# Attention streams of four groups: VectorE copies fills 0 and 1 of a round, ScalarE fills 2 and 3

## The chip, the cores and the metric

The kernel runs on one NeuronCore of a Trainium2 chip. The metric is the device time of one execution in microseconds (us); the time before is the median of three runs. A separate execution was recorded by the hardware profiler; all durations below come from it. PE is TensorE's matmul queue, PEld its weight loads, DVE is VectorE, ACT is ScalarE, POOL is GpSimd.

## The reference

The program is a stack of four pairs of an attention layer and a feed-forward layer over x of 8 x 256 x 256 (fp32), each normed first. Three of the four attention layers are touched. Cut to what they compute, per batch b of eight and head h:

```python
s = q[b, h] @ k[b, h].T (+ mask)      # 256 queries x keys
p = exp(s - max(s, axis=-1))
o = (p @ v[b, h]) / p.sum(-1)
x[b] += concat(o over h) @ Wp + bias
```

- ra (layer 0): 16 heads of 16, 256 keys, a mask of two classes and five register tokens that are treated on their own.
- ca (layer 1): 16 heads of 16, 512 keys (256 of the context, 256 of x itself).
- ma (layer 3): 8 heads of 32, 256 keys, masked.

## The kernel before, in words

All attention layers run through one generator, `attention_stream`. A stream is cut into rounds n = 0, 1, ... (NR of them, R for each batch). In a round four score units u = 0 to 3 are made, each a 128 x 512 block (128 queries by one head with 512 keys, or two heads with 256) in PSUM bank u. ra has 32 rounds, ca 64 (R = 8), ma 16 (R = 2). For each round:

- TensorE computes the four units (`scores`, L664; ra and ma add a mask product first, L660). Unit u may only be overwritten when ScalarE has taken the exponentials of the same unit of the round before (`exped`).
- VectorE takes the row maximum of each unit (`maxima`, L872). ScalarE takes the exponential of each (`exps`, L806) into prob. Where a unit has two heads, that is two exponentials.
- In the next round TensorE transposes prob (`turn(n-1, f)`, L678): a fill f is four 128 x 128 transposes that fill one PSUM bank. There are four fills in a round and two banks: fills 0 and 2 go to bank 4, fills 1 and 3 to bank 5. A fill is copied from PSUM to SBUF (pT) by `copy_turned`, on ScalarE L814, on VectorE L878. turn(., 2) waits until fill 0 has been copied, turn(., 3) until fill 1 has, turn(., 0) and turn(., 1) until fills 2 and 3 of the round before have.
- In every second round (odd n from 3) TensorE multiplies the transposed values of two rounds with v into bank 7 (`values`, L702).
- Other uses share bank 6, one after the other, at set places of a round: the projections of the next batch (front: L1187, L1203, in ma L1743, L1756, L1770), the output projection (L1161, L1791), the spread of the inverse sums (L721, copied by ScalarE at L828 and used by VectorE in `scale`, L900), in ra the register tokens (L745 to L760, with VectorE's L920 and ScalarE's L822).

Each engine has its own program, written out in full, and executes it in its order; engines meet only at semaphores. Nothing is reordered by a scheduler: the order of the calls in this function is the order on each engine. TensorE's order within a round n is

```
scores(n); shared slot 0; turn(n-1,0); turn(n-1,1); values or shared slot 1;
turn(n-1,2); turn(n-1,3); shared slot 1 if there were values; shared slot 2
```

and the change leaves it as it is. In ca the shared uses all lie in slot 1: fronts and output projection in even rounds between turns 1 and 2, the spread in rounds n%8 = 1 behind turn 3. `FILLS` is the number of fills in a round: 4 for ra, ca and ma (four groups), 2 for the streams na and pa, which keep their code.

Of the kernel before, what the change touches and what calls it, by code (L numbers as in the profile page):

```python
# [503 lines left out]
def attention_stream(g, ctx, tag, heads, dh, groups, keys, front, front_at, q_of, k_of, v_of, slot_of, project, finish,  # L504
# [12 lines left out]
    NR = B * R  # L517
# [4 lines left out]
    FILLS = NB  # L522
# [40 lines left out]
    def local(h):  # L563
        return h % HF

    def unit(n, u):
        r = n % R
        return (r % 2, u, groups[r // 2][u]) if GA == 4 else (u // 2, u % 2, groups[r][u % 2])

    def values_due(n):  # L570
        return 2 <= n <= NR + 1 and (n - 2) % VR == VR - 1
# [21 lines left out]
    def freer(use):  # L593
        if use[0] == "front":
            return front[use[2]][0]
        if use[0] == "reg":
            return ("a", "v", "v", "v")[use[2]]
        return {"project": "v", "spread": "a", "null": "a", "null_product": "v"}[use[0]]
# [15 lines left out]
    def shared_bank(use):  # L614
        n = ready_at[use] - 1
        return g.bank[n % 4] if n < len(first) else M

    with nc.Block() as block:
        @block.sync
        def _(sp):  # L620
            if n_loads:
                for b in range(B):
                    if b >= 2:
                        load_after(sp, b - 2, ready, ready_at, valued, R)
                    for d in load(sp, b):
                        d.then_inc(ld[b % 2], 16)
            sp.wait_ge(wl, 16 * n_weights)
# [16 lines left out]
        def _(pe):  # L644
# [24 lines left out]
            def turn(n, f):  # L669
                fill = FILLS * n + f  # L670
                last = f if NB == 4 else 2 * f + 1
                pe.wait_ge(exped, 4 * n + last + 1)
                if fill >= 2:
                    pe.wait_ge(copied_v if f % 2 == 0 else copied_a, (fill - 2) // 2 + 1)
                for j in range(4):
                    u, blk = (f, j) if NB == 4 else (2 * f + j // 2, j % 2)
                    c0 = (blk // KC) * keys + (blk % KC) * P
                    mm = pe.transpose(TB[f % 2][:, j * P:(j + 1) * P], prob[:, n % 2, u, c0:c0 + P], ident)  # L678
                mm.then_inc(turned, 1)
# [114 lines left out]
        @block.scalar  # L794
        def _(act):
            act.wait_ge(wl, 16 * n_weights)

            def exps(n, u):
                i, a, hs = unit(n, u)
                f = n // RF  # L800
                act.wait_ge(maxed, 4 * n + u + 1)
                if null is not None and n >= 2:
                    act.wait_ge(null_taken, n - 1)
                for hh in range(per):
                    hl = local(hs[hh])
                    e = act.activation(prob[:, n % 2, u, hh * keys:(hh + 1) * keys],  # L806
                                       S[u][:, hh * keys:(hh + 1) * keys], ACT.Exp, bias=nmax[:, n % 2, u, hh:hh + 1],
                                       accum_out=sums[:, f % 2, i, hl:hl + 1])
                e.then_inc(exped, 1)

            def copy_turned(n, f):
                act.wait_ge(turned, FILLS * n + f + 1)
                o = pT[:, n // 2 % 2, 4 * f:4 * f + 4, n % 2] if GA == 4 else pT[:, n % 2, :, f]
                act.activation(o, TB[f % 2][:].rearrange("p (j q) -> p j q", j=4), ACT.Copy).then_inc(copied_a, 1)  # L814

            def shared(use):
                if freer(use) != "a":
                    return
                bank = shared_bank(use)
                if use[0] == "reg":  # L820
                    act.wait_ge(reg_maxed, use[1] + 1)
                    e = act.activation(rp[:], bank[0:RN, 0:N], ACT.Exp, bias=rst[:, 0:1], accum_out=rst[:, 1:2])  # L822
                else:
                    act.wait_ge(ready, ready_at[use])
                    if use[0] == "front":
                        e = front[use[2]][2](act, bank, use[1])
                    elif use[0] == "spread":
                        e = act.activation(spreadS[:, use[1] % 2], bank[:], ACT.Copy)  # L828
                    else:
                        e = act.activation(pnT[:], bank[0:heads, 0:N], ACT.Copy)  # L830
                e.then_inc(freed_a, 1)

            for use in first:
                shared(use)
            for n in range(NR + 3):
                if n < NR:
                    exps(n, 0)
                    exps(n, 1)
                for use in slots[n][0]:
                    shared(use)  # L840
                if FILLS == 4:
                    if 1 <= n <= NR:
                        copy_turned(n - 1, 1)
                    if n < NR:
                        exps(n, 2)
                        exps(n, 3)
                    if not values_due(n):
                        for use in slots[n][1]:
                            shared(use)
                    if 1 <= n <= NR:  # L850
                        copy_turned(n - 1, 3)
                    if values_due(n):
                        for use in slots[n][1]:
                            shared(use)
                else:
                    if n < NR:
                        exps(n, 2)
                        exps(n, 3)
                    if 1 <= n <= NR:
                        copy_turned(n - 1, 1)  # L860
                    for use in slots[n][1]:
                        shared(use)
                for use in slots[n][2]:
                    shared(use)

        @block.vector
        def _(v):
            v.wait_ge(wl, 16 * n_weights)

            def maxima(n, u):  # L870
                v.wait_ge(scored, 4 * n + u + 1)
                v.tensor_reduce(nmax[:, n % 2, u], S[u][:, 0:W].rearrange("p (h k) -> p h k", h=per),  # L872
                                AX.X, ALU.max, negate=True).then_inc(maxed, 1)

            def copy_turned(n, f):
                v.wait_ge(turned, FILLS * n + f + 1)
                o = pT[:, n // 2 % 2, 4 * f:4 * f + 4, n % 2] if GA == 4 else pT[:, n % 2, :, f]
                v.tensor_copy(o, TB[f % 2][:].rearrange("p (j q) -> p j q", j=4)).then_inc(copied_v, 1)  # L878
# [28 lines left out]
            def reg_queries(b):  # L907
                wait_front(v, b)
                v.tensor_tensor(rq0[:], reg["q"](0, b), reg["q"](1, b), ALU.add).then_inc(reg_made, 1)
                v.wait_ge(reg_made, 3 * b + 1)  # L910
                for k in range(KD):
                    v.tensor_tensor(rq[:, k], rq0[:, k].unsqueeze(1).to_broadcast([P, 16, REG]),
                                    g.c("head16")[:, 16 * k:16 * k + 16].unsqueeze(2).to_broadcast([P, 16, REG]),
                                    ALU.mult).then_inc(reg_made, 1)
# [29 lines left out]
                shared(use)  # L944
            for n in range(NR + 3):
                if n < NR:
                    for u in range(2 if FILLS == 4 else 4):
                        maxima(n, u)
                    if reg is not None and n % R == 0:
                        reg_queries(n // R)  # L950
                for use in slots[n][0]:
                    shared(use)
                if 1 <= n <= NR:
                    copy_turned(n - 1, 0)
                if FILLS == 4:
                    if n < NR:
                        maxima(n, 2)
                        maxima(n, 3)
                    if not values_due(n):
                        for use in slots[n][1]:  # L960
                            shared(use)
                    if 1 <= n <= NR:
                        copy_turned(n - 1, 2)
                    if values_due(n):
                        for use in slots[n][1]:
                            shared(use)
                else:
                    for use in slots[n][1]:
                        shared(use)
                for use in slots[n][2]:  # L970
                    shared(use)
                if 1 <= n <= NR and (n - 1) % RF == RF - 1:
                    invert((n - 1) // RF)
                if 2 <= n <= NR + 1 and (n - 2) % RF == RF - 1:
                    scale((n - 2) // RF)
# [1272 lines left out]
```

## Time and profile before

| what | value |
|---|---|
| median of three runs | 2984.89 us (2981.12 to 2985.41) |
| the profiled execution, its time | 2986.86 us |
| its span in the profile | 2985.1 us |
| PE busy | 2450.5 us, 82% |
| DVE busy | 1213.5 us, 41% |
| ACT busy | 1049.7 us, 35% |
| ra stream, about | 290 to 566 us |
| ca stream, about | 600 to 953 us |
| ma stream, about | 2316 to 2512 us |

The span is the time between the first and the last recorded instruction; the execution's own time is 1.8 us longer. The streams that the diff touches take some 825 us of it. Busy shares are of the whole program, whose stages have different limits, so each stream has to be read for itself.

### The profile page before, as it was taken

To read this page: it belongs to the slowest core of one execution; us is meant where nothing else is said; L and a number is where in the kernel's file an instruction comes from. 1 tells how busy PE (TensorE), PEld (TensorE's weight loads), DVE (VectorE), ACT (ScalarE), POOL (GpSimd) and SP (SyncE) were. 2 spreads that over 40 slices of the span, in tenths; PEclk is the share of its full clock that TensorE was granted. 3 is DMA by queue.
4 is the path that set the end of the run, shared out by engine and by line. 5 is a ranking of instruction groups with operands and counts; after the bars stand their busy time and mean duration, and the time that the engine had idled before them with its cause. 6 is when DMAs were issued, how large, how long until landed. Compare 5 with 4: busy or idle time off the path is not lost. (4 is left out here: it accounts for less than half of the span.)

```text
span 2985.1 us, 39248 instructions
## 1 busy us (share of the span) xinstructions
PE 2450.5 (82%) x15064; PEld 1672.4 (56%) x15064; DVE 1213.5 (41%) x2325; ACT 1049.7 (35%) x2908; POOL 268.3 (9%) x323
## 2 busy tenths in 40 slices
PE   2464888789997589889899999997998997884894
PEld 2231556556665344444666666665786666664673
DVE  4234666577776221222333333334543444222003
ACT  1311556467775112221233333334321443322211
POOL 0000000000000123223000000002001000002003
PEclk9686999999999799999999999999999999887897
DMA  1100000000000200000200000000001000003332
GB/s 52 51 15 2 1 1 1 29 19 22 12 22 1 85 0 0 0 0 2 105 8 8 8 8 8 1 1 26 1 1 54 29 15 15 1 1 110 117 110 60
DMA packets 51018, 74.71 MB, mean 25 GB/s; under 512 B 8210, under 2 KB 40612, under 8 KB 49444
## 3 DMA queue, kind: packets, MB, share of 16 engines
q1 hardware_dynamic: 49316, 68.20, 6.7%
q0 software_dynamic: 1536, 4.20, 0.5%
q8 instruction: 116, 1.90, 0.3%
q14 instruction: 50, 0.41, 0.0%
HBM read 63.90 MB, written 8.39 MB: 24 GB/s over the span
## 5 line engine op out<-in xcount | busy, mean ns | idle before, releaser
L806 ACT ACTIVATE ca_prob<-bank,ca_nmax 128x512 f32<-128x512 f32 x256 | 174.2, 691 | 93.6 <-DVE ca_nmax L872 93.6
L872 DVE TENSOR_REDUCE ca_nmax<-bank 128x1 f32<-128x512 f32 x256 | 164.0, 682 | 57.0 <-PE bank L664 56.9
L1416 DVE TENSOR_TENSOR rf_hh<-rf_rc,rf_r 128x512 f32<-128x512 f32 x96 | 66.4, 692 | 293.1 <-POOL rf_rc L1322 293.1
L806 ACT ACTIVATE na_prob<-bank,na_nmax 128x257 f32<-128x257 f32 x256 | 118.1, 474 | 180.8 <-DVE na_nmax L872 180.8
L1355 PE MATMUL bank<-rf_xg,rf_W 128*128 128x512 f32 x384 | 179.1, 592 | 0.0
L1348 PE MATMUL bank<-rf_hh,rf_W 128*128 128x512 f32 x384 | 179.1, 592 | 0.0
L806 ACT ACTIVATE ra_prob<-bank,ra_nmax 128x256 f32<-128x256 f32 x256 | 118.4, 484 | 104.0 <-DVE ra_nmax L872 104.0
L678 PEld LDWEIGHTS bank<-cst,ca_prob 128*128 128x128 f32 x1024 | 112.1, 141 | 73.1 <-issue 63.7
L1322 POOL TENSOR_TENSOR rf_rc<-rf_r,rf_cw 128x512 f32<-128x512 f32 x96 | 124.4, 1296 | 286.2 <-ACT rf_r L1377 286.2
L1377 ACT ACTIVATE rf_r<-bank 128x512 f32<-128x512 f32 x96 | 57.3, 597 | 251.7 <-PE bank L1355 251.7
L678 PE MATMUL bank<-cst,ca_prob 128*128 128x128 f32 x1024 | 140.2, 279 | 6.0 <-DVE ca_pT L878 5.2
L872 DVE TENSOR_REDUCE na_nmax<-bank 128x1 f32<-128x257 f32 x256 | 90.8, 417 | 118.2 <-PE bank L664 118.2
L1348 PEld LDWEIGHTS bank<-rf_hh,rf_W 128*128 128x128 f32 x384 | 72.9, 190 | 91.9 <-issue 70.5
L1355 PEld LDWEIGHTS bank<-rf_xg,rf_W 128*128 128x128 f32 x384 | 72.6, 190 | 89.9 <-issue 89.9
L1603 PE MATMUL bank<-sf_h,sf_W 128*128 128x512 f32 x512 | 120.1, 395 | 0.0
L1485 PE MATMUL bank<-na_cxT,na_Wkv 128*128 128x256 f32 x512 | 118.5, 384 | 1.7 <-DVE na_q L1479 0.8
L1497 PE MATMUL bank<-na_Wkv,na_cxT 128*128 128x512 f32 x256 | 116.8, 601 | 3.3 <-ACT na_spread L828 2.6
L1603 PEld LDWEIGHTS bank<-sf_h,sf_W 128*128 128x128 f32 x512 | 95.9, 187 | 23.5
L1485 PEld LDWEIGHTS bank<-na_cxT,na_Wkv 128*128 128x128 f32 x512 | 95.0, 190 | 24.4 <-DVE na_q L1479 6.2
L664 PE MATMUL bank<-ca_k,ca_qz 32*128 32x512 f32 x512 | 73.9, 644 | 26.4 <-ACT ca_prob L806 25.6
L878 DVE COPY ca_pT<-bank 128x512 f32<-128x512 f32 x128 | 87.4, 683 | 16.4 <-PE bank L678 16.4
L237 PE MATMUL bank<-ln_rstd,cst 128*128 128x128 f32 x352 | 51.9, 291 | 49.8 <-DVE ln_rstd L311 49.8
(388 smaller groups left out, 4655.6 us busy)
## 6 DMA issues: line engine op xcount, KB each, us to landing
xl_w<-in_L_ffn_w SPq DMA_DIRECT2D x16, 1024.0 KB
rf_W<-in_L_ffn_w SPq DMA_DIRECT2D x2, 3072.0 KB, 14.4
dp_cx<-in_ctx_tok SPq DMA_DIRECT2D x4, 1024.0 KB, 5.5
ca_v<-in_ctx_values SPq DMA_DIRECT2D x8, 512.0 KB, 4.1
na_Wkv<-in_L_xattn_Wkv SPq DMA_DIRECT2D x1, 4096.0 KB
na_cxT<-in_ctx SPq DMA_DIRECT2D x8, 512.0 KB, 3.5
ma_cxT<-in_ctx SPq DMA_DIRECT2D x8, 512.0 KB, 3.5
X<-in_x SPq DMA_DIRECT2D x1, 2048.0 KB
```

Source lines behind the costliest of these rows:

```text
L664: mm = pe.matmul(S[u][:, hh * keys:(hh + 1) * keys], q_of(hs[hh], i, b), k_of(hs[hh], i, b), start=(mask is None), stop=(hh == per - 1), s ...
L678: mm = pe.transpose(TB[f % 2][:, j * P:(j + 1) * P], prob[:, n % 2, u, c0:c0 + P], ident)
L806: e = act.activation(prob[:, n % 2, u, hh * keys:(hh + 1) * keys], S[u][:, hh * keys:(hh + 1) * keys], ACT.Exp, bias=nmax[:, n % 2, u, hh: ...
L872: v.tensor_reduce(nmax[:, n % 2, u], S[u][:, 0:W].rearrange("p (h k) -> p h k", h=per), AX.X, ALU.max, negate=True).then_inc(maxed, 1)
L878: v.tensor_copy(o, TB[f % 2][:].rearrange("p (j q) -> p j q", j=4)).then_inc(copied_v, 1)
L1322: po.tensor_tensor(rc[:, c % 3], r[:, c % 3], cw[:, expert[c]], ALU.mult).then_inc(rcd, 1)
L1348: mm = pe.matmul(g.bank[6 + m][:], W2[:, c, m * P:(m + 1) * P], hh[:, c % 3], start=(c == 0), stop=(c == CH - 1), skip_group_check=True)
L1355: mm = pe.matmul(g.bank[2 + c % 3][:], W1[:, k, c * P:(c + 1) * P], xg[:, k], start=(k == 0), stop=(k == KD - 1))
L1416: v.tensor_tensor(hh[:, c % 3], rc[:, c % 3], r[:, c % 3], ALU.mult).then_inc(hd, 1)
L1485: mm = pe.matmul(bank[:, m * N:(m + 1) * N], Wkv[:, k, (m0 + m) * P:(m0 + m + 1) * P], cxT[:, b % 2, k], start=(k == 0), stop=(k == KC - 1))
L1497: mm = pe.matmul(bank[:], cxT[:, b % 2, k, t * P:(t + 1) * P], Wkv[:, k, INNER + half * 512:INNER + (half + 1) * 512], start=(k == 0), sto ...
L1603: mm = pe.matmul(g.bank[m % 4][:], W1[:, k, m * P:(m + 1) * P], h[:, k, s], start=(k == 0 and s == 0), stop=(k == C1 - 1 and s == 1))
```

## The change

In streams with four fills VectorE now copies fills 0 and 1, and ScalarE fills 2 and 3; before, VectorE had 0 and 2, ScalarE 1 and 3. VectorE takes three maxima, copies fill 0, takes the fourth maximum and copies fill 1. ScalarE takes all four exponentials in a row, and then copies fills 2 and 3. TensorE's waits are adapted: turns 2 and 3 wait for VectorE's copies of the same round, turns 0 and 1 for ScalarE's copies of the round before. The number of instructions is the same.

```diff
@@ turn(n, f), TensorE
                 pe.wait_ge(exped, 4 * n + last + 1)
-                if fill >= 2:
+                if FILLS == 4 and f >= 2:
+                    pe.wait_ge(copied_v, 2 * n + f - 1)
+                elif FILLS == 4 and n >= 1:
+                    pe.wait_ge(copied_a, 2 * n + f - 1)
+                elif FILLS == 2 and fill >= 2:
                     pe.wait_ge(copied_v if f % 2 == 0 else copied_a, (fill - 2) // 2 + 1)
@@ ScalarE
                 if FILLS == 4:
-                    if 1 <= n <= NR:
-                        copy_turned(n - 1, 1)
                     if n < NR:
                         exps(n, 2)
                         exps(n, 3)
...
                     if 1 <= n <= NR:
+                        copy_turned(n - 1, 2)
                         copy_turned(n - 1, 3)
@@ VectorE
-                    for u in range(2 if FILLS == 4 else 4):
+                    for u in range(3 if FILLS == 4 else 4):
                         maxima(n, u)
...
                 if FILLS == 4:
                     if n < NR:
-                        maxima(n, 2)
                         maxima(n, 3)
+                    if 1 <= n <= NR:
+                        copy_turned(n - 1, 1)
                     if not values_due(n):
                         for use in slots[n][1]:
                             shared(use)
-                    if 1 <= n <= NR:
-                        copy_turned(n - 1, 2)
```

VectorE in one round of ca (n%8 = 1), before; ca_nmax is the maximum of the unit in banks 0 to 3, the copies read the banks of the fills, and L900 is the scale behind the round:

```order
L872 TENSOR_REDUCE ca_nmax<-bank0 128x1
L872 TENSOR_REDUCE ca_nmax<-bank1 128x1
L878 COPY ca_pT<-bank4 128x4x128
L872 TENSOR_REDUCE ca_nmax<-bank2 128x1
L872 TENSOR_REDUCE ca_nmax<-bank3 128x1
L878 COPY ca_pT<-bank4 128x4x128
L900 TENSOR_TENSOR ca_outT<-bank7,ca_spread 128x512
```

The same round after the change (the lines have moved by a few):

```order
L875 TENSOR_REDUCE ca_nmax<-bank0 128x1
L875 TENSOR_REDUCE ca_nmax<-bank1 128x1
L875 TENSOR_REDUCE ca_nmax<-bank2 128x1
L881 COPY ca_pT<-bank4 128x4x128
L875 TENSOR_REDUCE ca_nmax<-bank3 128x1
L881 COPY ca_pT<-bank5 128x4x128
L903 TENSOR_TENSOR ca_outT<-bank7,ca_spread 128x512
```

The second copy stands at the same place, sixth in the round, but it now reads bank 5 (fill 1) and not bank 4 (fill 2); the maximum of bank 2 has moved ahead of the first copy.

ScalarE in the same round, before; ca_prob are the exponentials, and L828 copies the spread:

```order
L806 ACTIVATE ca_prob,ca_sums<-bank0,ca_nmax 128x512
L806 ACTIVATE ca_prob,ca_sums<-bank1,ca_nmax 128x512
L814 ACTIVATE ca_pT<-bank5 128x4x128
L806 ACTIVATE ca_prob,ca_sums<-bank2,ca_nmax 128x512
L806 ACTIVATE ca_prob,ca_sums<-bank3,ca_nmax 128x512
L814 ACTIVATE ca_pT<-bank5 128x4x128
L828 ACTIVATE ca_spread<-bank6 128x512
```

and after:

```order
L810 ACTIVATE ca_prob,ca_sums<-bank0,ca_nmax 128x512
L810 ACTIVATE ca_prob,ca_sums<-bank1,ca_nmax 128x512
L810 ACTIVATE ca_prob,ca_sums<-bank2,ca_nmax 128x512
L810 ACTIVATE ca_prob,ca_sums<-bank3,ca_nmax 128x512
L818 ACTIVATE ca_pT<-bank4 128x4x128
L818 ACTIVATE ca_pT<-bank5 128x4x128
L832 ACTIVATE ca_spread<-bank6 128x512
```

The copy of fill 1 between the second and the third exponential is gone, and the copy of fill 2 stands behind the fourth.

## Rows read from the trace of the kernel before

**Rows 1.** Windows: engine, us busy (x instructions), granted clock, DMA share, GB/s

```profile
694.00:737.00 43.00, 40.09 (x362) 26.96 (x361) 33.44 (x57) 31.46 (x82) 0.55 (x2) 1.00 0.06 20
...
611.00:614.00 3.00, 2.63 (x11) 1.16 (x12) 0.55 (x1) 0.71 (x3) 0.00 (x0) 0.56 0.00 0
```

**Rows 2.** Tile ca_prob, who waited for it: us in total, times

```profile
  PE bank L664: 25.6, 56
```

**Rows 3.** Timeline, ca, a common round: start us, us, what [idle before]

```profile
746.80 1.14 PE L664 MATMUL bank<-ca_k,ca_qz 32*128 32x512 f32 x8 [0.71 <-ACT ca_prob L806]
...
747.93 1.29 DVE L872 TENSOR_REDUCE ca_nmax<-bank 128x1 f32<-128x512 f32 x2 [0.81 <-PE bank L664]
748.65 0.69 ACT L806 ACTIVATE ca_prob<-bank,ca_nmax 128x512 f32<-128x512 f32 x1 [1.51 <-DVE ca_nmax L872]
...
749.13 0.68 DVE L878 COPY ca_pT<-bank 128x512 f32<-128x512 f32 x1
...
749.73 1.28 DVE L872 TENSOR_REDUCE ca_nmax<-bank 128x1 f32<-128x512 f32 x2
...
750.00 0.59 ACT L814 ACTIVATE ca_pT<-bank 128x512 f32<-128x512 f32 x1
750.47 0.69 ACT L806 ACTIVATE ca_prob<-bank,ca_nmax 128x512 f32<-128x512 f32 x1
...
751.14 0.70 ACT L806 ACTIVATE ca_prob<-bank,ca_nmax 128x512 f32<-128x512 f32 x1
...
752.07 1.14 PE L664 MATMUL bank<-ca_k,ca_qz 32*128 32x512 f32 x8 [0.22 <-ACT ca_prob L806]
```

**Rows 4.** Timeline, ca, a turn that waited for VectorE's copy

```profile
926.67 0.68 DVE L878 COPY ca_pT<-bank 128x512 f32<-128x512 f32 x1
...
927.50 0.63 PE L678 MATMUL bank<-cst,ca_prob 128*128 128x128 f32 x4 [1.00 <-DVE ca_pT L878]
```

**Rows 5.** Timeline of PE, ca, rounds n%8 = 1 and 2

```profile
907.64 1.14 PE L664 MATMUL bank<-ca_k,ca_qz 32*128 32x512 f32 x8 [0.71 <-ACT ca_prob L806]
...
912.53 1.06 PE L721 MATMUL bank<-cst,ca_wide 128*128 128x128 f32 x8
913.51 1.14 PE L664 MATMUL bank<-ca_k,ca_qz 32*128 32x512 f32 x8
...
919.06 1.14 PE L664 MATMUL bank<-ca_k,ca_qz 32*128 32x512 f32 x8 [0.71 <-ACT ca_prob L806]
```

**Rows 6.** Timeline of PE, ra, from turn 3 to the next round

```profile
305.68 0.63 PE L678 MATMUL bank<-cst,ra_prob 128*128 128x128 f32 x4 [0.63 <-ACT ra_pT L814]
306.23 0.65 PE L660 MATMUL bank<-ra_km,ra_qm 2*128 2x512 bf16 x3
```

**Rows 7.** Timeline, ra, first and second round of a batch

```profile
398.53 0.41 DVE L920 TENSOR_REDUCE ra_rst<-bank 80x1 f32<-80x256 f32 x1
...
399.87 0.47 ACT L822 ACTIVATE ra_rp<-bank,ra_rst 80x256 f32<-80x256 f32 x1
...
402.51 1.41 DVE L1194 TENSOR_SCALAR ra_qz<-bank,cst 128x512 f32<-128x512 f32 x2 [2.97 <-PE bank L1187]
...
404.36 1.28 DVE L872 TENSOR_REDUCE ra_nmax<-bank 128x2 f32<-128x512 f32 x2
...
408.11 1.06 PE L721 MATMUL bank<-cst,ra_wide 128*128 128x128 f32 x8
...
409.64 0.66 ACT L828 ACTIVATE ra_spread<-bank 128x512 f32<-128x512 f32 x1
```

**Rows 8.** Timeline, ra, fourth round of a batch

```profile
420.52 1.29 DVE L872 TENSOR_REDUCE ra_nmax<-bank 128x2 f32<-128x512 f32 x2 [0.70 <-PE bank L664]
...
423.31 1.13 PE L678 MATMUL bank<-cst,ra_prob 128*128 128x128 f32 x8
424.28 0.51 PE L760 MATMUL bank<-cst,ra_ro 80*128 80x5 f32 x4
```

**Rows 9.** Timeline of PE, ca, near its start

```profile
611.37 2.09 PE L664 MATMUL bank<-ca_k,ca_qz 32*128 32x512 f32 x8 [0.71 <-ACT ca_prob L806]
```

## The prediction

> **What bounds the kernel now.** I read the groups by line first, then the windows of the three streams that the diff touches (ra 290 to 566 us, ca 600 to 953, ma 2316 to 2512), then the timeline of single rounds. The largest is ca, with 64 rounds. In a steady stretch of it TensorE is busy 40.09 of 43 us at a granted clock of 1.00 [rows 1], so about 2.9 us in eight rounds can be won at most. Its idle time is one wait: the score products L664 waited for the exponentials of the round before, 25.6 us in 56 waits [rows 2].
>
> A common round of ca shows why [rows 3]. Counted from the start of the scores at 746.80: the first maximum starts 1.13 later, the first exponential 0.72 after that, the second fill's copy on ScalarE (L814) 1.35 after that, the third exponential 0.47 later, the fourth 0.67 later, and the next scores 0.93 later, at 752.07. The sum is 5.27 us, a loop from TensorE over VectorE and ScalarE back to TensorE, with 0.22 us of TensorE idle at its end. In other rounds the idle time is larger but the period is the same. Six of eight rounds run so. Round n%8 = 1, which ends in the spread product L721, takes 5.87 us (907.64 to 913.51) and has no wait ahead of the scores: there TensorE itself is the limit. The next takes 5.55 (to 919.06), since VectorE scales the output first [rows 5].
>
> **What the change does.** The number of instructions stays. Per round, the copy of fill 1 goes from ScalarE to VectorE, behind the fourth maximum; the copy of fill 2 goes the other way, behind the fourth exponential; the third maximum passes the copy of fill 0. In ca this makes two loops where one was.
>
> *The exponential loop.* Exponentials no longer wait for a copy. On VectorE two maxima take 1.20 and a copy 0.60 [rows 3], so the fourth maximum starts 1.13 + 1.80 + 0.60 = 3.53 after the scores, the fourth exponential 0.72 later and the next scores 0.93 after it: 5.18 us. ScalarE alone would allow 1.13 + 0.72 + 1.35 + 0.67 + 0.93 = 4.80, so the fourth maximum is what holds. By this loop the round wins only 0.09 of the 0.47 us that the copy cost.
>
> *The copy loop.* TensorE runs turn(n-1,3) ahead of scores(n+1), and turn 3 fills the bank that the copy of fill 1 empties. Before, that was ScalarE's copy at 750.00, 3.20 after the scores, early enough that TensorE's idle time lay at the scores and not at turn 3. Now it is VectorE's sixth instruction of the round: 1.13 + 3 x 0.60 + 0.60 + 0.60 = 4.13 after the scores. From the start of a VectorE copy to the turn that waited for it are 0.83 us (926.67 to 927.50) [rows 4], so turn 3 starts at 4.96. From a turn to the scores behind it: 0.55 in ra (305.68 to 306.23) [rows 6], where a mask product follows; half of a pair of turns is 0.49 (423.31 to 424.28) [rows 8]. I take 0.52 between them. The period becomes 4.96 + 0.52 = 5.48, longer by 0.21 than now. Everything of this loop is serial: maxima and copies stand back to back on VectorE, and the next maxima need the next scores.
>
> The Trainium skill (TensorE: Matmul & The Clock Gate, Part 2) says that TensorE pulls only weight loads ahead, and matmuls stay in program order. By that rule scores(n+1) cannot pass a waiting turn 3; if they could, the round would go by the 5.18 loop. In the rows here no score product stands ahead of its turns.
>
> The sum for ca, of 62 intervals with fills:
> - 48 common rounds x 0.21 = 10.1 us.
> - 7 spread rounds: turn 3 at 4.96, spread product 0.49 later, scores 0.98 after it (912.53 to 913.51) [rows 5] = 6.43 instead of 5.87: 0.56 x 7 = 3.9 us. Here TensorE had no slack, so the wait is all loss.
> - 7 rounds behind them: the scale is late by as much as the scores, the rest is as in a common round: 0.21 x 7 = 1.5 us.
>
> Together 15.5 us. The front products of the even rounds hide none of it: they stand between turns 1 and 2 and end before 4.96. What VectorE does for them now comes behind the copy of fill 1, from 4.73 on; the longest (query take and reciprocal, in ra 1.85 us from 402.51 to 404.36 with one instruction more [rows 7]) ends by 6.58, while the next maximum can start at 5.48 + 1.13 = 6.61; this cover is thin, but a batch has one such round. The late copies on ScalarE: turn 3 starts at 4.96, its transposes take 0.63 [rows 6], the copy 0.59 [rows 3] and the release about 0.15, as behind VectorE's (0.83 less 0.68 [rows 4]): the bank is free at 6.33; turn 1 of the next round wants it at 5.48 + 1.07 + 0.5 = 7.0. Hidden by 0.7 us, and by some 0.4 where the keys' copy is queued there too.
>
> *ra*, by batches of four rounds. Round 0: the register maximum L920 moves from 398.53 to 399.13; L822 waits for it and for the fourth exponential (both about 399.6) instead of starting at 399.87 behind the extra copy: 0.25 us won, since the front product waits for L822. Round 1 starts 0.25 earlier, at a first maximum of 404.11; copy of fill 1 at 407.11, turn 3 at 407.94, spread product at 408.43 (was 408.11), the spread's copy 1.09 behind that, 409.52 (was 409.64) [rows 7]: 0.12 still won. Round 2 waits for nothing that moved. Round 3: first maximum 420.52 - 0.12 = 420.40, turn 3 at 424.23, the next product L760 at 424.72 instead of 424.28 [rows 8]: 0.44 lost, and the chain over L760 to the next scores passes it on. About 7.5 batches x 0.44 = 3.2 us. *ma*: its even rounds are set by long front and project products, no cost; its odd ones are like ra's round 1 without the 0.25 ahead: 0.13 x 7 = 0.9 us. No bound from below excludes zero for these two.
>
> Sum: 15.5 + 3.2 + 0.9 = 19.6 us. The profiled execution took 2986.86 us, so it would give 3006.5; the median of the runs, 2984.89, lies 2.0 below it, so 3004.5.
>
> **Rivals.** Clear of the noise of this measurement is what differs by over 0.2%, 6 us.
>
> *A. The copy loop does not bind (faster).* If the stretch from the start of the copy of fill 1 to the next scores were under 5.18 - 4.13 = 1.05 us instead of 0.83 + 0.52 = 1.35, the exponential loop would set the period: 55 x -0.09 = -5.0 in ca, -0.12 x 8 = -1.0 in ra, the spread rounds unchanged: 2979. For it: the present profile names only the exponentials as what TensorE waits for [rows 2]. Against: both pieces are measured, and 0.3 us is far over their spread. 4%.
>
> *B. Parts cancel (no change).* The copy loop binds by a little, ra and ma win in round 0 and lose nowhere: from 2979 to 2991. It needs the period at 5.33 or less. 5%.
>
> *C. TensorE's clock falls in ca.* At 611 to 614 the granted clock was 0.56 on average [rows 1], after a few idle stretches, and the scores took 2.09 instead of 1.14 us at 611.37 [rows 9]: 0.95 us a fall. Now 43 us with 2.9 idle run at 1.00; then about 5 in 45 (6 x 5.48 + 6.43 + 5.76). One fall in each batch of eight would add 8 x 0.95 = 7.6: 3012. 10%. The Trainium skill (TensorE: Matmul & The Clock Gate, "A second HAM failure mode") has a kernel whose short idle stretches between matmul groups made the clock swing; by that rule the new waits in every round could do it. The present rounds, with idle stretches of 0.22 and more in almost each, do not show it.
>
> *D. ScalarE's two late copies hold up the next turns.* The 0.4 to 0.7 us of slack would have to be gone; at 0.2 us a round, 12 us more: 3017. 3%.
>
> **How the numbers follow.** The forecast has 78%, A 4%, B 5%, C 10%, D 3%. Low end: turn to scores 0.47 and 0.03 less for the release (62 x 0.08 = 5 off), nothing in ra and ma (4 off): 2995. High end: C's price on top: 3012. Faster 0.04, same 0.05, slower 0.91.
>
> **What the profile after would show.** In ca: scores every 5.48 us; the group of turns L682 idle in front of turn 3, waiting for VectorE's ca_pT, some 0.4 us in common rounds and 0.5 in spread rounds; hardly any wait of L664 for ca_prob; the exponentials without a gap for a copy, then both copies; spread rounds 6.43. In ra, L822 a quarter of a us earlier and turn 3 late in rounds 1 and 3. I am wrong if the turns wait for ca_prob or for ScalarE, if the period is under 5.33, or if the clock in ca is below 0.99.

## The result and the profile after

The changed kernel takes 3003.11 us (median of seven runs, 2992.07 to 3007.39), the kernel before 2982.51 (median of seven, 2976.74 to 2985.41). The ratio is 1.0068, with a 95% interval of 1.0052 to 1.0084, so the change costs about 20 us (15.5 to 25). The forecast was 3004.5 us, slower. The profiled execution of the changed kernel took 3002.29 us, its span is 3000.5.

The page's row of busy times, which answers to the table on the kernel before:

```profile
PE 2456.2 (82%) x15064; PEld 1660.0 (55%) x15064; DVE 1209.0 (40%) x2325; ACT 1061.6 (35%) x2908; POOL 268.6 (9%) x323
```

The busy times moved little (TensorE 5.7 us more, ScalarE 11.9 more, VectorE 4.5 less): what has changed is who waits. The windows view of nearly eight rounds of ca, as in [rows 1]:

```profile
748.00:791.00 43.00, 39.11 (x327) 24.95 (x324) 30.58 (x53) 30.80 (x77) 0.50 (x1) 1.00 0.06 19
```

TensorE is now busy 39.11 of 43 us, where it was 40.09, and the granted clock is still 1.00. The tile view of ca_prob, first what TensorE's turns waited for, then who waited for the exponentials (us, times), against [rows 2]:

```profile
  DVE ca_pT L881: 37.5, 68
...
  PE bank L664: 1.8, 1
```

The 56 waits of the scores L664 for an exponential are one, and in their place are 68 waits of the turns L682 for VectorE's copy, 37.5 us instead of 25.6. The timeline of a common round of ca, against [rows 3] (start, duration, what, idle time before):

```profile
767.40 1.14 PE L664 MATMUL bank<-ca_k,ca_qz 32*128 32x512 f32 x8
...
768.55 1.89 DVE L875 TENSOR_REDUCE ca_nmax<-bank 128x1 f32<-128x512 f32 x3 [1.86 <-PE bank L664]
...
769.28 0.69 ACT L810 ACTIVATE ca_prob<-bank,ca_nmax 128x512 f32<-128x512 f32 x1 [0.91 <-DVE ca_nmax L875]
...
770.36 0.68 DVE L881 COPY ca_pT<-bank 128x512 f32<-128x512 f32 x1
...
770.96 0.68 DVE L875 TENSOR_REDUCE ca_nmax<-bank 128x1 f32<-128x512 f32 x1
...
771.55 0.68 DVE L881 COPY ca_pT<-bank 128x512 f32<-128x512 f32 x1
...
772.35 1.29 ACT L818 ACTIVATE ca_pT<-bank 128x512 f32<-128x512 f32 x2
772.38 0.63 PE L682 MATMUL bank<-cst,ca_prob 128*128 128x128 f32 x4 [0.37 <-DVE ca_pT L881]
...
772.94 1.14 PE L664 MATMUL bank<-ca_k,ca_qz 32*128 32x512 f32 x8
```

The period is 5.54 us (767.40 to 772.94), it was 5.27. It is the copy loop of the prediction: the first maximum 1.15 after the scores, five VectorE instructions in 3.00, the second copy at 771.55, the turn that it releases 0.83 later, and the scores 0.56 behind that turn, without a wait of their own. The spread round and the one behind it, in TensorE's timeline, against [rows 5]:

```profile
789.57 1.14 PE L664 MATMUL bank<-ca_k,ca_qz 32*128 32x512 f32 x8
...
794.55 0.63 PE L682 MATMUL bank<-cst,ca_prob 128*128 128x128 f32 x4 [0.37 <-DVE ca_pT L881]
795.02 1.06 PE L725 MATMUL bank<-cst,ca_wide 128*128 128x128 f32 x8
796.01 1.14 PE L664 MATMUL bank<-ca_k,ca_qz 32*128 32x512 f32 x8
```

6.44 us instead of 5.87; the round behind it takes 5.79 instead of 5.55. At two places the clock fell as well. This is the later one, where an even round has no front product between its turns:

```profile
924.27 0.63 PE L682 MATMUL bank<-cst,ca_prob 128*128 128x128 f32 x4 [1.62 <-DVE ca_pT L881]
925.46 1.08 PE L682 MATMUL bank<-cst,ca_prob 128*128 128x128 f32 x4 [0.57 <-DVE ca_pT L881]
926.48 2.09 PE L664 MATMUL bank<-ca_k,ca_qz 32*128 32x512 f32 x8
...
933.87 1.14 PE L664 MATMUL bank<-ca_k,ca_qz 32*128 32x512 f32 x8
```

After idle stretches of 1.62 and 0.57 us the turn and the scores run at the lower of the two clock levels, 1.2 GHz (2.09 us instead of 1.14, as in [rows 9]), and the spread round takes 7.39 instead of 6.44. In ra, against [rows 7] and [rows 8]: L826 (L822 before) in the first round of a batch, the front product behind it, and turn 3 of the fourth round of that batch:

```profile
395.75 0.39 PE L660 MATMUL bank<-ra_km,ra_qm 2*128 2x512 bf16 x4 [1.45 <-DVE ra_vz L1215]
...
401.58 0.47 ACT L826 ACTIVATE ra_rp<-bank,ra_rst 80x256 f32<-80x256 f32 x1
...
402.20 1.99 PE L1189 MATMUL bank<-XN,ra_Wqkv 128*128 128x256 f32 x8 [0.20 <-ACT ra_rp L826]
...
426.10 0.63 PE L682 MATMUL bank<-cst,ra_prob 128*128 128x128 f32 x4 [0.38 <-DVE ra_pT L881]
426.57 0.51 PE L764 MATMUL bank<-cst,ra_ro 80*128 80x5 f32 x4
```

L826 starts 5.83 us after the round's mask product; before, it was 6.13. In the fourth round turn 3 waits where it did not wait.

Worked out from the starts of the score products, in us:

| stretch | before | after |
|---|---|---|
| ca: common, spread, behind it | 5.27, 5.87, 5.55 | 5.54, 6.44, 5.79 |
| ca, first to last scores | 338.88 | 359.17 |
| ca, to the next norm's first product | 356.28 | 377.03 |
| ra, the four rounds of a batch | 8.66, 8.24, 8.59, 9.25 | 8.38, 8.27, 8.59, 9.79 |
| ra, first three intervals; last three | 24.17; 20.11 | 25.15; 20.74 |
| ma, even and odd round | 13.43, 12.50 | 13.46, 12.50 |

Against before, and each up to the first product of the norm behind it, ca takes 20.75 us more, ra 4.06 and ma 0.91: 25.7. The two executions are only 15.4 apart (3002.29 - 2986.86), so code that the diff does not touch was 10.3 us shorter. Most of it, 9.3 us, lies behind ma's last scores, and the largest piece there is the stream pa. Windows over the same work, before and then after:

```profile
2541.00:2671.00 130.00, 111.35 (x576) 78.49 (x575) 35.51 (x87) 35.20 (x141) 3.68 (x6) 0.85 0.00 1
```

```profile
2564.20:2687.90 123.70, 104.85 (x576) 73.71 (x574) 35.45 (x87) 34.93 (x141) 3.69 (x6) 0.90 0.00 1
```

The same 576 matmuls take 6.5 us less TensorE time at a clock of 0.90 than at 0.85. The norms behind ra and ma are shorter in the same way (29.79 to 27.20 us at 0.89 and 1.00; 26.32 to 24.71 at 0.85 and 0.93), the one behind ca longer (21.04 to 22.71 at 1.00 and 0.92).

### The profile page after: what moved, and what is told of

It is laid out like the page before. It is cut to its first block and busy times, and to the rows that moved or that the text cites. A ratio compares the mean times of both kernels' runs of the same rounds, so it can differ in the third digit from the quotient of the medians.

```text
span 3000.5 us, 39248 instructions
## 1 busy us (share of the span) xinstructions
PE 2456.2 (82%) x15064; PEld 1660.0 (55%) x15064; DVE 1209.0 (40%) x2325; ACT 1061.6 (35%) x2908; POOL 268.6 (9%) x323
## 5 line engine op out<-in xcount | busy, mean ns | idle before, releaser
L682 PE MATMUL bank<-cst,ca_prob 128*128 128x128 f32 x1024 | 152.5, 282 | 38.8 <-DVE ca_pT L881 37.5
L682 PEld LDWEIGHTS bank<-cst,ca_prob 128*128 128x128 f32 x1024 | 109.3, 141 | 123.8 <-issue 110.2
L875 DVE TENSOR_REDUCE ra_nmax<-bank 128x2 f32<-128x512 f32 x128 | 82.1, 683 | 22.8 <-PE bank L664 22.8
L1492 ACT ACTIVATE na_k<-bank 128x512 f32<-128x512 f32 x32 | 19.2, 599 | 203.0 <-PE bank L1487 203.0
```

## The experiments

The theory: the period of ca is the serial way scores, three maxima, copy of fill 0, fourth maximum, copy of fill 1, turn 3, scores. The first rival says that the exponentials of the round before still hold the scores, and the waits at the turns are only where the idle time is shown; the second that the third maximum ahead of the copy, or ScalarE's two late copies, cost the time. Each kernel's time is given with its ratio to the kernel before, which ran on the same chip.

### 1. Finer waits for the exponentials, in the changed kernel and in the one before

TensorE waited for the exponential of each unit ahead of all four units' products. In ca the wait now stands directly in front of the product that overwrites the unit. The same edit was made in both kernels.

```diff
-                        if n > 0:
+                        if n > 0 and mask is not None:
                             pe.wait_ge(exped, 4 * (n - 1) + u + 1)
...
                             i, a, hs = unit(n, u)
+                            if n > 0 and mask is None and hh == 0:
+                                pe.wait_ge(exped, 4 * (n - 1) + u + 1)
                             mm = pe.matmul(S[u][:, hh * keys:(hh + 1) * keys], ...
```

> The changed kernel, but in ca each score product waits only for the exponential of its own unit (before it, all four waits stood ahead of the first product). Theory (copy loop: maxima, copy 0, maximum, copy 1 on VectorE, then turn 3, then the scores): nothing that binds is touched, the common round of ca stays at 5.54 us (5.50 to 5.56), about 3000 us in all. Rival (the scores are held by the exponentials, at least in part): the common round falls to 5.0 to 5.3 us, 15 to 30 us less than the changed kernel.

> The kernel before with the same edit of the waits. Theory: before the change the round was held by the fourth exponential, ahead of all four score products; with waits by unit the first product goes behind turn 3 at once and the fourth exponential hides behind the first three, so the common round falls from 5.27 to what TensorE needs, 5.0 to 5.1 us: about 12 us less than before, 2970. Rival (the round is held by something else, such as VectorE's maxima or TensorE's turns): 5.27 stays, and the time with it.

In the changed kernel: 3001.17 us, ratio 1.0067 (1.0042 to 1.0091), and ca rounds of 5.54, 6.44 and 5.79, all as without the edit. The very first interval is shorter, 2.99 instead of 4.82, and the two clock falls of the changed kernel are missing: the rounds that took 6.00 and 7.39 there take 5.54 and 6.44 here. Its timeline of a common round:

```profile
738.42 1.14 PE L666 MATMUL bank<-ca_k,ca_qz 32*128 32x512 f32 x8
...
743.40 0.63 PE L684 MATMUL bank<-cst,ca_prob 128*128 128x128 f32 x4 [0.57 <-DVE ca_pT L883]
743.96 1.14 PE L666 MATMUL bank<-ca_k,ca_qz 32*128 32x512 f32 x8
```

In the kernel before: 2967.02 us, ratio 0.9955 (0.9937 to 0.9973). Timeline of two common rounds (n%8 = 3 and 4):

```profile
740.54 0.70 ACT L808 ACTIVATE ca_prob<-bank,ca_nmax 128x512 f32<-128x512 f32 x1
740.70 1.81 PE L666 MATMUL bank<-ca_k,ca_qz 32*128 32x512 f32 x8
...
741.38 0.29 PEld L666 LDWEIGHTS bank<-ca_k,ca_qz 32*128 32x128 f32 x2 [0.38 <-ACT ca_prob L808]
...
746.35 1.14 PE L666 MATMUL bank<-ca_k,ca_qz 32*128 32x512 f32 x8
...
751.04 1.21 PE L666 MATMUL bank<-ca_k,ca_qz 32*128 32x512 f32 x7
```

The scores start at 740.70, while the last exponential of the round before (740.54) is under way; the last units' weight loads wait for it, 0.38 us, and the whole product takes 1.81 instead of 1.14. Common rounds now mostly alternate: 4.70 for even n, 5.47 for odd n, and 5.65 for n%8 = 3. The spread round grew from 5.87 to 6.38 and the one behind it fell from 5.55 to 4.77, so that eight rounds take 41.8 us instead of 43.1; from the first to the last scores ca takes 326.3 instead of 338.9. So exponentials bound the round before and do not bound it after: the same edit gains 0.45% there and nothing here. The rival of the exponentials is out for the changed kernel. The kernel before with this edit is the fastest of all those in this document.

### 2. Only the third maximum ahead of the copy

From the kernel before; VectorE takes three maxima ahead of the copy of fill 0, and nothing else moves.

```diff
-                    for u in range(2 if FILLS == 4 else 4):
+                    for u in range(3 if FILLS == 4 else 4):
                         maxima(n, u)
...
                     if n < NR:
-                        maxima(n, 2)
                         maxima(n, 3)
```

> The kernel before with one part of the change alone: VectorE takes the third maximum ahead of the copy of fill 0; who copies what is as before. Theory: no loop that binds in ca goes through it (fill 0 has to be copied for turn 2, which TensorE reaches later; ScalarE stands at its copy when the third maximum is ready), so the common round stays at 5.27 us and the time within 3 us of before. Rival (the late copy of fill 0 holds turn 2): 5.35 to 5.9 us a round, 5 us and more slower.

2981.39 us, ratio 1.0006 (0.9989 to 1.0024). The scores in TensorE's timeline:

```profile
744.86 1.14 PE L664 MATMUL bank<-ca_k,ca_qz 32*128 32x512 f32 x8
...
750.41 1.14 PE L664 MATMUL bank<-ca_k,ca_qz 32*128 32x512 f32 x8 [0.45 <-ACT ca_prob L806]
```

This is the round behind a spread, 5.55 as before; the common ones are 5.27, those of ma and, but for one, of ra unchanged. In ra the register queries now stand behind three maxima: TensorE idles 1.54 us ahead of L745 in each batch (0.94 before), in one of them the clock then fell and the round took 0.66 more, and the first three intervals cost 25.02 instead of 24.17. That is nearly all of the 0.98 that the whole change costs there. In the time of the kernel this part of the change can't be told from nothing; what costs in ca is which engine copies fills 1 and 2, and when.

### 3. The copy of fill 1 ahead of the third and fourth maximum

From the changed kernel. VectorE: two maxima, copies of fills 0 and 1, two maxima. The copy is 1.2 us earlier, but the last maxima, and so the last exponentials, come behind both copies. If the order on VectorE sets the round, the exponentials must be the limit again, at a longer period.

```diff
-                    for u in range(3 if FILLS == 4 else 4):
+                    for u in range(2 if FILLS == 4 else 4):
...
                         copy_turned(n - 1, 0)
+                        copy_turned(n - 1, 1)
                     if n < NR:
+                        maxima(n, 2)
                         maxima(n, 3)
-                    if 1 <= n <= NR:
-                        copy_turned(n - 1, 1)
```

> The changed kernel with VectorE's order maximum, maximum, copy 0, copy 1, maximum, maximum. Theory: the copy loop shrinks to 4.35 us and the exponential loop takes over, since the fourth maximum is now the sixth instruction: 1.15 + 5 x 0.60 + 0.72 + 0.93 = 5.80, or by the third exponential 5.87; the common round of ca is 5.80 to 5.90 us, ca some 15 us longer than in the changed kernel. Rival (what costs is that ScalarE's copies come late, or that VectorE copies two fills in a row at all): the round stays at 5.54. A second rival (turn 3 alone costs, the exponentials have slack): it falls below 5.3.

3041.8 us, ratio 1.0207 (1.0177 to 1.0238). Timeline of a common round:

```profile
802.22 1.14 PE L664 MATMUL bank<-ca_k,ca_qz 32*128 32x512 f32 x8 [1.07 <-ACT ca_prob L810]
...
804.55 1.28 DVE L881 COPY ca_pT<-bank 128x512 f32<-128x512 f32 x2
...
805.75 1.28 DVE L875 TENSOR_REDUCE ca_nmax<-bank 128x1 f32<-128x512 f32 x2
...
807.14 0.68 ACT L810 ACTIVATE ca_prob<-bank,ca_nmax 128x512 f32<-128x512 f32 x1
...
808.06 1.14 PE L664 MATMUL bank<-ca_k,ca_qz 32*128 32x512 f32 x8 [0.79 <-ACT ca_prob L810]
```

5.84 us, and the wait is back at the scores, for ScalarE's ca_prob. With four maxima and two copies in one queue, whatever stands last sets the round, a maximum by way of the exponentials or a copy by way of the turn; of these two orders that of the change is the shorter. ca is 15.7 us longer than in the changed kernel; ra (10.1 more, with several clock falls) and ma (6.5 more) make up most of the rest of the 39.

### 4. All four maxima ahead of both copies

From the changed kernel: `for u in range(4)`, and the `maxima(n, 3)` behind the copy of fill 0 goes. The copy of fill 1 stays sixth on VectorE.

> The changed kernel with VectorE's order maximum x4, copy 0, copy 1. Theory: the copy of fill 1 is still the sixth instruction, so the common round of ca stays at 5.54 us although the fourth exponential can start 0.6 us earlier; turn 2 waits too, now, but hands on within the wait of turn 3. The time is within 4 us of the changed kernel's. Rival (the exponentials have a part in the loss): 5.2 to 5.4 us a round, about 10 us less than the changed kernel.

3018.0 us, ratio 1.0123 (1.0082 to 1.0164). The ca rounds are 5.54, 6.44 and 5.79, exactly those of the changed kernel: in ca only the place of the copy of fill 1 counts, not what stands in front of it. But the time is 15 us above the changed kernel's, where at most 4 were expected. In the two profiled executions 17.0 us lie between the spans, and 7.8 of them are in ra, where the scores' span grew from 265.9 to 273.6 us. There the register queries L912 to L915 now stand behind four maxima. TensorE's timeline in the first round of two batches:

```profile
402.69 0.27 PE L749 MATMUL bank<-ra_km,ra_rmask 2*80 2x256 bf16 x1 [2.14 <-DVE ra_rq L915]
402.89 1.82 PE L751 MATMUL bank<-ra_k,ra_rq 128*80 128x256 f32 x4
```

```profile
475.82 0.27 PE L749 MATMUL bank<-ra_km,ra_rmask 2*80 2x256 bf16 x1 [2.14 <-DVE ra_rq L915]
476.02 1.09 PE L751 MATMUL bank<-ra_k,ra_rq 128*80 128x256 f32 x4
```

In both TensorE idles 2.14 us ahead of L749 (the changed kernel 1.54). In the second the round takes 8.74 instead of 8.38; in the first the clock falls on top, L751 takes 1.82 instead of 1.09 and the round 9.92. Three batches went the one way and three the other: 3 x 0.36 + 3 x 1.55 = 5.7 of the 7.8 us; the other 2.1 are in the first and last intervals of the stream. The rest of the 17 is from the last scores of ra to the first of ca (4.3), in clock falls in ca (1.7) and behind the last scores of ma (3.4).

### 5. A filler of 0.2 us between the fourth maximum and the second copy, in both kernels

A memset of a tile that nobody reads, on VectorE, once a round of the four-group streams. If the loop of the theory binds, each common round grows by the filler's step; if VectorE has slack, as it should in the kernel before, by nothing.

```diff
+                        v.memset(pad[:, n % 4], 0.0)     # pad = sb("pad", [P, 4, 256]), behind maxima(n, 3)
```

> The changed kernel with a memset of 128x256 fp32 of a spare tile between the fourth maximum and the copy of fill 1 on VectorE, in every round with a fourth maximum. It adds work that the reference does not have. Theory: VectorE stands in the loop without slack, so each common round of ca grows by the whole step of the memset (0.15 to 0.35 us by size): 5.7 to 5.9, and ca by about 60 times as much. Rival (VectorE has slack, the loss comes from ScalarE's side): 5.54 stays.

> The kernel before with the same memset at the same place, between the fourth maximum and the copy of what is there fill 2. It adds work that the reference does not have. Theory: there VectorE's sixth instruction is in no loop, so the common round of ca stays at 5.27 us, and the time within 3 us of before. Rival (VectorE's load as such sets the round): it grows by the step of the memset as in the changed kernel.

In the changed kernel: 3024.08 us, ratio 1.0154 (1.0107 to 1.02). Its timeline:

```profile
737.76 1.14 PE L665 MATMUL bank<-ca_k,ca_qz 32*128 32x512 f32 x8
...
742.00 0.27 DVE L962 MEMSET ca_pad<- 128x256 f32 x1
742.20 0.63 DVE L882 COPY ca_pT<-bank 128x512 f32<-128x512 f32 x1
...
742.97 0.63 PE L683 MATMUL bank<-cst,ca_prob 128*128 128x128 f32 x4 [0.79 <-DVE ca_pT L882]
743.53 1.14 PE L665 MATMUL bank<-ca_k,ca_qz 32*128 32x512 f32 x8
```

The filler takes 0.20 us of VectorE's queue, and the rounds are 5.76, 6.66 and 6.01: 0.22 more each. In the kernel before: 2981.93 us, ratio 1.0002 (0.9988 to 1.0016):

```profile
744.97 1.14 PE L665 MATMUL bank<-ca_k,ca_qz 32*128 32x512 f32 x8 [0.71 <-ACT ca_prob L807]
...
749.18 0.27 DVE L960 MEMSET ca_pad<- 128x256 f32 x1
...
750.24 1.14 PE L665 MATMUL bank<-ca_k,ca_qz 32*128 32x512 f32 x8 [0.21 <-ACT ca_prob L807]
```

5.27 again; only the spread round went from 5.87 to 5.94. There VectorE's copy of fill 2 stands behind the filler and the two query takes of the front product. It started 0.33 us after the scores (before: 0.16), and the turn that it releases 0.82 behind it, 1.15 after the scores and not 1.07: VectorE had slack, but in this one round not quite 0.2 us. The same instruction costs its full length in every round once VectorE is in the loop, and next to nothing when it is not.

### 6. The changed kernel once more

> The changed kernel once more. Theory: the three streams take the same time again (ca's common round 5.54, spread round 6.44, the one behind it 5.79), while stages that the change does not touch differ by some us with the granted clock, above all the layer behind ma, which was 7.7 us shorter in the profile of the changed kernel than in that of before. Rival (the change shortens that layer): it is as short again, within 1 us.

One execution with a profile: 3002.94 us. The rounds of ca, ra and ma are the same as in the first profile, with the two clock falls of ca at the same rounds. pa took 121.9 us at a clock of 0.92, not 123.7 at 0.90, which is the third value for this code (130.0 before). By itself this looks like a stretch that varies with the granted clock and not with the change. The other profiles say otherwise. Windows over the whole of pa, in the kernel before, in the kernel before with the filler, and in the changed kernel:

```profile
2537.16:2696.40 159.24, 133.25 (x769) 96.42 (x770) 43.92 (x112) 42.62 (x167) 6.62 (x13) 0.86 0.00 1
```

```profile
2538.90:2697.40 158.50, 133.10 (x769) 96.70 (x769) 44.04 (x112) 42.70 (x166) 6.60 (x13) 0.86 0.00 1
```

```profile
2562.10:2713.40 151.30, 125.04 (x769) 90.38 (x770) 43.99 (x112) 42.45 (x166) 6.63 (x13) 0.92 0.00 1
```

The four kernels that copy the fills as before (these two, and those of experiments 1 and 2 that start from the kernel before) take 158.5 to 159.3 us, all at 0.86. The six profiles in which VectorE copies fills 0 and 1 take 144.9 to 156.8, at 0.88 to 0.96. The groups do not overlap, so the shorter pa goes with the change, by way of the clock, although no instruction of pa was touched; how the change reaches it no run shows. The clock accounts for the length. This is a window of the kernel with the filler, over the same part of pa as the two in the result:

```profile
2584.40:2697.40 113.00, 94.14 (x574) 67.01 (x574) 35.24 (x87) 34.80 (x141) 3.67 (x6) 1.00 0.00 1
```

113.0 us at 1.00 in this kernel, which was slower as a whole, and 129.9 at 0.85 in the fastest one (experiment 1, on the kernel before). A change can be paid back, or paid for once more, in code that it does not touch, and a stage's length says little unless its clock stands beside it.

## Why the prediction was right, step by step

- **What bound the kernel before: right.** The loop over the exponentials. Finer waits for them gain 14 us there, and a filler on VectorE costs next to nothing.
- **The copy loop takes its place: right.** 5.54 us where 5.48 was forecast. Its pieces were 1.15 (forecast 1.13), 3.00 (3.00), 0.83 (0.83) and 0.56 (0.52). The last is the one that was mis-sized: I took it between two rows of other operations behind a turn, 0.55 and 0.49, and with the scores of ca behind it, it is at the upper one. Experiment 5 shows that the loop is serial (0.20 put in, 0.22 out), experiments 3 and 4 that the place of the copy of fill 1 on VectorE decides.
- **Spread rounds 6.43, rounds behind them 5.76: right** (6.44 and 5.79). The waits at turn 3 are 0.57 us in even and 0.37 in odd rounds, the spread rounds included, where 0.4 and, for spread rounds, 0.5 were forecast.
- **The sum for ca, 15.5 us, was too small.** Measured 20.75. By the measured rounds it is 48 x 0.27 + 7 x 0.57 + 7 x 0.24 = 18.6. Clock falls add 1.8: rounds of 5.93, 6.49, 6.00 and 7.39 are over the others by 0.39, 0.95, 0.46 and 0.95, where the kernel before had one of 0.95. Between 18.6 and 15.5 lies mostly the 0.06 of the common round, times 48.
- **ra, 3.2 us: near as a sum (4.06), which is partly luck; its parts are less so.** Round 0 won 0.28 (0.25), round 3 lost 0.54 (0.56 against the new start of the round, 0.44 for the batch). Round 1 grew by 0.03 only, where 0.13 of the win was to be lost, so its chain over the spread is shorter than I had it; that step was mis-sized by 0.10. With rounding a batch costs 0.28 and not 0.44. Against that, the first and last three intervals of the stream, which I had counted as half a batch, cost 0.98 and 0.63; by experiment 2 the 0.98 comes nearly all from the third maximum, a term that the sum did not have.
- **ma, 0.9 us: the size is right (0.91) by luck, the mechanism is not.** The cost was to be in the odd rounds, by the late turn 3. Odd rounds did not move (12.50), even rounds grew by 0.03, and 0.6 came in a single interval (8.84 to 9.45) near the stream's start.
- **Rival A, the copy loop does not bind: out**, by experiments 1 and 5. **B, parts cancel: out.** The win in ra's round 0 is real and gone in round 3.
- **Rival C, clock falls in ca: happened, but not as a pattern.** It was to be one fall in each batch of eight. There were two where the kernel before had one, about 1.8 us more in all, both behind even rounds without a front product, where TensorE idles 1.62 and 0.57 us in one round. With 0.37 or 0.57 us of idle time a round the clock stayed at 1.00. The Trainium skill (TensorE: Matmul & The Clock Gate, "A second HAM failure mode") has a kernel whose short idle stretches made the clock swing; the idle stretches of common rounds here did not, the longer ones at these two places and those of 2.14 us in experiment 4 did, though not each time. The round ahead of the first of the two had stretches of 1.60 and 0.57 and no fall behind it, and in the changed kernel of experiment 1 the same two rounds, with 1.63 and 0.57, had none either. So how long the idle stretch was does not by itself tell whether a fall follows.
- **Rival D, ScalarE's late copies hold the turns: out.** No turn of ca waited for L818 in the changed kernel's views of waits.
- **What was missing from the sum: the streams and the whole do not differ by the same.** The streams lost 25.7 us in the profiled pair, the medians 20.6, the profiled pair 15.4. The forecast of 19.6 was 6 us short on the streams, and it met the medians because untouched code came out shorter, a term that it did not have. That it lies about 1 us from the measured 20.6 is luck; that the change costs, and by which loop, is not. The windows show that the shorter code goes with a higher clock in pa, in every profile with the new distribution of copies (section 6 of the experiments); by what way stays open.

By the Trainium skill (TensorE: Matmul & The Clock Gate, Part 2) matmuls stay in program order and only weight loads are pulled ahead. The trace agrees: in ca the scores always stand behind turn 3, 0.56 us, and turn 3 carries the waits.

## What to carry to other kernels

Before moving an instruction between engines, write down every loop through the in-order queues with the position of each instruction in it, and not only the loop that binds: taking a 0.47 us copy out of the exponentials' loop would by the prediction's sum have been worth 0.09 us (no run shows that loop alone), while the same copy as VectorE's sixth instruction released its PSUM bank almost a microsecond later and closed a loop that was longer. The place of a copy that frees a bank, in the queue of whichever engine makes it, is a price of its own; but moving it to the front is no rule, for in experiment 3 it stood 1.2 us earlier and the maxima behind it cost more (5.84 us a round and not 5.54). Where exponentials are what the scores wait for, a wait belongs directly in front of the instruction that has the hazard and not ahead of its group: that edit alone, on the kernel before, gave 0.9955 (0.9937 to 0.9973), and on the changed kernel nothing.

## What was not expected of the hardware

The same code of pa, 574 to 576 matmuls without a change, took 113.0, 118.0, 121.9, 123.7 and 130.0 us at granted clocks of 1.00, 0.95, 0.92, 0.90 and 0.85, and the four kernels with the old distribution of copies all had the lowest clock there. And one extra idle stretch of 0.6 us on TensorE (2.14 instead of 1.54, experiment 4) cost 0.36 us in three batches and 1.55 in three others of one execution, the difference being a fall of the clock. With 1.54 us there was a fall in one batch of experiment 2 and in none of the changed kernel.
